# Down weights of all eight experts kept on the chip, addressed by a register of TensorE

## The reference

```
x = x + 0.5 * ffn(layernorm(x));  x = x + attn(layernorm(x));  x = x + 0.5 * ffn(layernorm(x))
x = x + 0.5 * experts(x);         x = x + linear_attn(x);      x = x + 0.5 * experts(x)

def experts(x):
    xn = x * rsqrt(mean(x * x, -1) + eps) * ln_w
    vals, idx = top_k(xn @ Wg + bg, 2)
    w = softmax(vals)                       # the two weights of each row
    for e in range(8):                      # out starts at 0
        y = (silu(xn @ W1a[e] + b1a[e]) * (xn @ W1b[e] + b1b[e])) @ W2[e] + b2[e]
        out += weight_of_e_in_row * y
```

## Time and profile before

| | |
|---|---|
| median of 3 runs | 887.13 us (885.59 to 891.52) |
| the profiled execution | 894.74 us |
| its span, first to last instruction | 892.9 us |
| TensorE busy | 676.6 us, 76% of the span |
| first expert layer, tile loop | about 502 to 642 us |
| second expert layer, tile loop | about 735 to 875 us |

### The profile page before, as it was taken

The page is one execution under the profiler, slowest core; times in us unless marked ns, Lnnn a source line. Parts: engine busy times, 40 slices in busy tenths (PEclk is TensorE's granted clock), DMA queues, the critical chain, the costliest instruction groups (busy, mean ns, idle before and its releaser), DMA issues.

```text
span 892.9 us, 13483 instructions
## 1 busy us (share of the span) xinstructions
PE 676.6 (76%) x4694; PEld 502.3 (56%) x4694; DVE 486.9 (55%) x1449; ACT 441.4 (49%) x867; POOL 331.9 (37%) x393
## 2 busy tenths in 40 slices
PE   4498897479999993387996498889639657988981
PEld 2266784312222242265896488778537656878870
DVE  7878749821111129877748245435557753444553
ACT  6365314589999978254306333323424642333440
POOL 1390312213223213361303546545340063656443
PEclk8589999779999998599997599989959877999996
DMA  8100000585000000000002745547230056655544
GB/s 338 45 0 1 1 1 1 189 268 206 2 1 1 1 1 4 0 1 1 1 1 54 245 150 169 167 146 216 73 94 1 1 142 217 195 159 173 173 145 150
DMA packets 35688, 83.36 MB, mean 93 GB/s; under 512 B 5025, under 2 KB 19873, under 8 KB 35105
## 3 DMA queue, kind: packets, MB, share of 16 engines
q1 hardware_dynamic: 30496, 71.87, 24.5%
q0 software_dynamic: 5120, 10.58, 4.2%
HBM read 65.62 MB, written 16.81 MB: 92 GB/s over the span
## 4 chain that ended last, share of the span: by engine, by line
PE 55%; DVE 21%; issue 10%; ACT 9%; DMA 3%; POOL 1%; SPq 0%; DVEq 0%; ACTq 0%
PE ps L1918 17%; PE ps L1929 8%; PE ps L1830 5%; PE ps L1599 3%; ACT arena L1410 3%; PE ps L1725 3%; PE ps L1813 3%; DVE arena L705 2%; PE ps L1697 2%; DVE arena L703 2%; PE ps L1706 1%; DVE stats L610 1%; DVE arena L782 1%; PE ps L1837 1%; PE ps L1905 1%
## 5 line engine op out<-in xcount | busy, mean ns | idle before, releaser
L1918 PE MATMUL ps<-arena 128*128 128x256 f32 (+1 forms) x768 | 165.6, 370 | 36.1 <-issue 33.0
L1918 PEld LDWEIGHTS ps<-arena 128*128 128x128 f32 x768 | 135.9, 206 | 56.5 <-issue 37.2
L1466 ACT ACTIVATE arena<-ps,arena 128x256 f32<-128x256 f32 (+1 forms) x192 | 83.6, 438 | 166.2 <-PE ps L1918 73.3
L955 DVE SCALAR_TENSOR_TENSOR arena<-ps,arena 128x256 f32<-128x256 f32 (+1 forms) x192 | 83.8, 439 | 126.7 <-ACT arena L1466 104.2
L1410 ACT ACTIVATE arena<-ps 128x512 f32<-128x512 f32 (+3 forms) x192 | 138.4, 827 | 4.5 <-PE ps L1813 3.2
L583 POOL DMA_INDIRECT yd<-arena,wq x80 | 78.6, 983 | 114.7 <-DVE arena L977 100.0
L547 POOL DMA_INDIRECT arena<-xs,wq x80 | 77.7, 971 | 31.3 <-issue 21.0
L1830 PE MATMUL ps<-arena 128*32 128x512 f32 (+3 forms) x768 | 83.6, 507 | 2.4 <-DVE arena L1188 1.6
L535 POOL TENSOR_SCALAR_AFFINE_SELECT arena<-arena 128x512 f32<-128x512 f32 x64 | 40.6, 634 | 115.0 <-ACT arena L1410 115.0
L1929 PE MATMUL ps<-arena 128*128 128x128 f32 x640 | 79.9, 276 | 2.0 <-DVE arena L977 2.0
L1929 PEld LDWEIGHTS ps<-arena 128*128 128x128 f32 x640 | 75.8, 193 | 2.5 <-issue 2.4
(11 more groups left out here) (295 smaller groups left out, 1288.0 us busy)
## 6 DMA issues: line engine op xcount, KB each, us to landing
arena<-in_wall SPq DMA_DIRECT2D x48, 836.0 KB
arena<-scr_q SPq DMA_DIRECT2D x8, 512.0 KB, 6.8
arena<-scr_k SPq DMA_DIRECT2D x8, 512.0 KB, 7.9
arena<-yd SPq DMA_DIRECT2D x8, 512.0 KB, 5.3
xs<-Xn SPq DMA_DIRECT2D x8, 260.0 KB, 4.9
scr_q<-arena SPq DMA_DIRECT2D x4, 384.0 KB, 4.5
scr_k<-arena SPq DMA_DIRECT2D x4, 384.0 KB, 3.9
arena<-xs,wq POOLq DMA_INDIRECT x80
```

The lines of the kernel that those rows point to most:

```text
L955: nc.vector.scalar_tensor_tensor(out=hT[:, j % 2, f, 0:rows], in0=ps[:, 3 + k % 3, 0:rows], scalar=raw[:, slot, EW_BB + f:EW_BB + f + 1], ...
L1466: nc.scalar.activation(sl[:, k % 3, 0:rows], ps[:, k % 3, 0:rows], ACT.Silu, bias=raw[:, slot, EW_BA + f:EW_BA + f + 1]).then_inc(sem("sil ...
L1918: ins = mm(ps[:, bank, 0:rows], raw[:, slot, w + P * f:w + P * (f + 1)], xTt[:, j % 2, 0:rows], start=True, stop=True)
```

## The change

The down weights of all eight experts leave the expert's load and are kept on the chip: one load of 128 x 4096 words (2 MB), at the start of the first expert layer, brings them into the last words of the arena (`kept`), where they stay for both layers. The load of each tile shrinks from 1672 to 1160 words for each partition (580 KB for 836 KB); the last bias stays in it. TensorE now reads the tile's expert from `tab` into a register of its own ahead of each down product and uses it in the address of the moving operand. It waits once a layer for the table and for the kept load. The semaphore `gatep` becomes the first count of `rank`.

```diff
-EW_A, EW_B, EW_2, EW_BA, EW_BB, EW_B2, EW = 0, 512, 1024, 1536, 1540, 1544, 1672
+EW_A, EW_B, EW_BA, EW_BB, EW_B2, EW = 0, 512, 1024, 1028, 1032, 1160
+EW_KEPT = 512
...
+        kept = arena[:, ARENA - E_ * EW_KEPT:ARENA].rearrange("p (e w) -> p e w", e=E_)
...
                 if not before:
                     sp.dma_start(route, a["route"]).then_inc(sem("route_in"), 16)
+                    sp.dma_start(kept[:, :, :], a["kept"]).then_inc(sem("kept_in"), 16)
                 sp.wait_ge(*at("expgap", i, 2))
...
-                gates(3).then_inc(sem("gatep", i), 1)
+                gates(3).then_inc(sem("rank", i), 1)
...
                 def down(j):
-                    slot = (before * NTILE + j) % WSLOT
+                    expert = pe.value_load(tab[0:1, j:j + 1], min_val=0, max_val=E_ - 1)
                     pe.wait_ge(*at("h", i, FT * (j + 1)))
                     if j:
                         pe.wait_ge(*at("y", i, j))
                     for h in range(TILES[j][1]):
                         for f in range(FT):
                             ins = mm(ps[:, 6, D * h:D * (h + 1)], hT[:, j % 2, f, P * h:P * (h + 1)],
-                                     raw[:, slot, EW_2 + D * f:EW_2 + D * (f + 1)], start=(f == 0), stop=(f == FT - 1))
+                                     kept[:, bass.ds(expert, 1), D * f:D * (f + 1)].rearrange("p o w -> p (o w)"), start=(f == 0), stop=(f == FT - 1))
                     ins.then_inc(sem("down", i), 1)
 
                 rows_in(0)
+                pe.wait_ge(*at("table", i, 1))
+                pe.wait_ge(sem("kept_in"), 16)
...
+    kept = z(P, E_, EW_KEPT)
...
-    wall[:, :, EW_2:EW_2 + FT * D] = f("L1_ffn_W2").reshape(E_, FT, P, D).transpose(2, 0, 1, 3).reshape(P, E_, FT * D)
+    kept[:, :, 0:FT * D] = f("L1_ffn_W2").reshape(E_, FT, P, D).transpose(2, 0, 1, 3).reshape(P, E_, FT * D)
```

More of the change, by code:

```diff
@@ L123 @@
                 nullv_in=16),
-    "moe": dict(gatep=1, pick=2, rank=2, columns=2, distance=len(PICK_ACT), act_rows=len(PICK_ACT), rows=4, index=2, counts=1, passed=7, expgap=2, mix=1, table=1,
+    "moe": dict(pick=2, rank=3, columns=2, distance=len(PICK_ACT), act_rows=len(PICK_ACT), rows=4, index=2, counts=1, passed=7, expgap=2, mix=1, table=1,
                 stored_rows=16 * NC, xtp=NTILE, xt=NTILE, up=NTILE * FT, silu=NTILE * FT, h=NTILE * FT,
@@ L873, in moe @@
                 backwards = over(route[:, RC_REV:RC_REV + E_], NT)
-                dve.wait_ge(*at("gatep", i, 1))
+                dve.wait_ge(*at("rank", i, 1))
                 link(nc.vector.tensor_tensor(lg, ps[:, 4, 0:NT * E_].rearrange("p (t e) -> p t e", t=NT),
@@ L895, in moe @@
                 nc.vector.tensor_tensor(mix[:, :, 1], mix[:, :, 0], gw[:, 1, :], ALU.mult).then_inc(sem("mix", i), 1)
-                dve.wait_ge(*at("rank", i, 1))
+                dve.wait_ge(*at("rank", i, 2))
                 rank_ = ps[:, 6, 0:NT * E_].rearrange("p (t e) -> p t e", t=NT)
@@ L936, in moe @@
                         ins.then_inc(sem("rows", i), 1)
-                dve.wait_ge(*at("rank", i, 2))
+                dve.wait_ge(*at("rank", i, 3))
                 nc.vector.tensor_copy(total, ps[:, 5, 0:COLS])
@@ L2096, in _layout @@
         "wall": wall,
+        "kept": kept,
         "route": route,
```

## The result

The changed kernel took 899.06 us (median of 4 runs, 896.9 to 901.5), the kernel before 886.36 us beside it: a ratio of 1.013, 95% interval 1.0099 to 1.0161. The forecast was 865, and the result lies above its range (850 to 893). The profiled execution took 896.9 us (span 895.1), only 2.2 us more than that of before, since it is one of the fastest of its kernel and the other lies above the four runs of its own. Besides, its trace has a head start of 2.9 us from steps in which nothing was changed: the route table's load starts at 467.37 us, before at 470.25. So the two traces show how the stages differ and the ratio shows by how much.

What follows compares the result with a forecast made beforehand. Bound: TensorE stalled on late signals, blamed on GpSimd transfers queued behind weight loads. Terms -23.4 - 5 + 0 + 0 + 6 = -22.4 us from 894.74 give 872.3; the runs' median, 7.6 lower, gives 865 us, range 850 to 893.

Steps and rivals of the forecast that it cites:

- The failing step: Wide tiles 4 to 16: shorter loads land transfers before GpSimd's fifth issue, so late signals stop; -23.4 us, ends -23.4 and 0.
- the run decides, not the bytes: Rival, wide tiles: GpSimd issuing more than four in a row makes signals late, however soon they land; 893 us, chance 0.17.
- The sentence against it: Against that rival: first gather's landing (5.09 us) and fifth issue (5.16) coincide so closely that bytes must matter.
- The layer starts: Start of each expert layer, six loads and 11 gathers competing: part of 11.6 us standing time goes; -5 us, ends -10.5 and 0.
- Narrow tiles by register work: Down products of 14 narrow tiles: register work exposes 0.3 to 0.5 us each; +6 us, between +1 and +11.
- Wide tiles hide it: Wide tiles' down products: 0.45 to 0.8 us of register work a tile is hidden behind 3.62 us of up product; no cost.
- the slower rival: Four matmuls of each down product: register addresses make them sent more slowly than the array takes them; 905 us, chance 0.11.
- The kept load: 2 MB load on SP's queue ahead of the sorted rows' stores: takes 7.8 us in an idle stretch, costs nothing.
- The merged semaphore: Merged semaphore and two waits ahead of the loop: a few tens of nanoseconds, counted as 0.

Runs made afterwards that it cites:

- late: Kind of comparison in which the kernel before takes 886 to 894 us, its trace showing stalls ahead of wide tiles' up products.
- few_bytes_2: Kernel before with weight loads of tiles 6 to 23 of each layer cut to 4 KB: 1.0052 late; as few_bytes, 0.9985 prompt.
- big_load: Changed kernel with each tile's load padded again to 836 KB, registers and kept weights as changed, against the kernel before: 1.0052 prompt.
- static_expert_2: Changed kernel with down product at expert 0's fixed address, no TensorE register work, against the kernel before: 0.9971 late; as static_expert, 0.9938 prompt.
- fewer_gathers: Kernel before with the second of two gathers left out in wide tiles 7 to 16, against the kernel before: 0.9729 late, 865.96 us.
- prompt: Kind of comparison in which the same kernel before takes 847 us; no trace of an edited kernel there has a wide-tile stall.
- early_one: Kernel before with EARLY = 1, SP waiting for tile 0's rows after one weight load, not two, against the kernel before: 0.9940 prompt.
- register_load_alone: Kernel before with an unused register load and its check ahead of each TensorE down product, against the kernel before: 1.0060 prompt.
- load_only: Changed kernel with register load kept but matmuls at expert 0's fixed address, against the kernel before: 1.0002 prompt; repeat 1.0023 late.
- hoisted_load_2: Changed kernel with the register load moved ahead of the next tile's up product, against the kernel before: 1.0079 late; earlier 0.9975 prompt.
- changed_fewer_gathers: Changed kernel without the second gather of wide tiles 7 to 16, against the kernel before: 1.0005 prompt; repeat 0.9734 late.

## Why the prediction was wrong

**The failing step** is in the first part of the change: "Then never more than three are out, and the late signals stop", the -23.4 us. Bytes do delay GpSimd's transfers (5.46 us against 3.66 for the first gather), but that delay doesn't make signals late. With loads of 4 KB the stalls stand (few_bytes_2), and with 836 KB loads and the same issues they can be absent (big_load). What the runs showed in its place: the stalls stay at 580 KB (27.9 us in tiles 2 to 16 for 23.7, and 21.4 in static_expert_2, where by the forecast nearly all should have gone), and those of the wide tiles go when GpSimd issues three transfers a tile and not four (fewer_gathers, 24 us). The rival "the run decides, not the bytes" was nearer. It isn't the whole of it: in prompt comparisons eleven issues in a row do no harm. The sentence against it, that landing and fifth issue coincide too closely, took 5.09 against 5.16 us for evidence, from a single gather. By the rule of the Trainium skill ("DMA: Bandwidth & Descriptors", "Queues, rings and completion order") that a DMA engine takes turns between its queues packet by packet I had put down that rival's time. The result (899 us) was nearer to that (893), though no run shows that it was for this reason: a gather did wait longer beside longer loads, 5.46 us for 3.66.

**The layer starts**, -5: about right as a sum, for another reason. The standing time after the first up product stayed (5.20 and 6.40 us before, 5.08 and 7.42 after in the timelines); the first gather landed 1.3 us earlier in the second layer's chain. static_expert (0.9938) puts the term at some 5 us, early_one (0.9940), which touches only when the first loads start, has as much. It goes with the loads' length: with the same register load on TensorE register_load_alone (836 KB) is at 1.0060 and load_only (580 KB) at 1.0002, both prompt. That the size was right is luck, since the reason given for it, fewer late signals, was wrong.

**Narrow tiles by register work**, +6: 14 x (3.50 - 3.06) = 6.2 us if every narrow tile pays it. In prompt traces tiles 17 to 22 of both layers, twelve of the fourteen, take 43.7 us (big_load) for 38.5 (few_bytes), 5.2 more: the term was right. The trace has 0.30 us for the load, 0.15 for the operation behind it and 0.046 for each of the four at the matmuls; I had estimated 0.27 to 0.48 and up to 0.165. The floor of about 600 ns that the Trainium skill gives for a loaded value ("DMA: Bandwidth & Descriptors", "Latency and other measured facts") is twice the 302 ns of this trace, which decides.

**Wide tiles hide it**: right where nothing is late (5.46 us in big_load with all register work), so the slower rival, matmuls that are sent too slowly, is refuted. Beside late signals it doesn't hold: 27.9 to 32.5 us lost against 21.4 for the fixed address, and 10.8 us between hoisted_load_2 and static_expert_2, whose narrow tiles without a stall are alike (3.07 and 3.06 us). That term, about 1% (1.0079 against 0.9971), stood at nothing in the prediction and was in no rival.

**The kept load**, 7.8 us and hidden: it took 7.9, in the idle stretch, and the stores behind it weren't held up. **The merged semaphore**: nothing of it shows.

**The sum as measured**, prompt: about -5 for the starts, +5 to 6 for the narrow tiles, 0 for the rest, and changed_fewer_gathers has 1.0005. Late: +12.7 us by the medians for a forecast of -22.4. The 23.4 us of stalls didn't go, and about 1% came on top of the prompt sum. In the traces of the three runs of the changed kernel the two tile loops, up to the last tile's up product, take 273.4, 278.8 and 280.5 us for 268.3: 4.1 to 8.7 us more in tiles 2 to 16, 1.4 to 4.7 in tiles 17 to 22, and 0.2 to 1.3 less in tiles 0 and 1. Each is one execution, so where the whole of the 1% lies isn't shown more closely.

**What stays open.** The traces show where late and prompt comparisons differ, but not what makes them differ. Rate, number in flight and bytes of GpSimd's transfers weren't told apart. And why register work lengthens the stalls was not settled; the operations wait for the loaded value and, as the order shows, for h and y too, so a signal that is late may be paid twice on TensorE's sequencer, but that is only argued. No kernel with fewer issues and the whole computation was run, so nothing here shows that the 24 us can be had.

## What to carry to other kernels

Idle time whose releaser the profile can't name should be tested by one kernel that takes the suspected cause away altogether, before a change is built on it: loads of four kilobytes in place of 836 settled here, in the first late comparison, what the traces could not. Ask also whether the stall is the kernel's own: compare executions from more than one occasion. A value loaded ahead of short work was paid in full (0.29 us on a tile of 3.06, 0.43 with the operations that use it), so it belongs one block of work earlier. The first transfer of a stage should share the engines with as few loads as the stage can bear: with one less it landed 2.1 us sooner (3.36 for 5.46 us), and the next tile's weights came 1.85 us late.

## What the hardware showed that was not expected

The same kernel ran at 847 or at 886 to 894 us, 5%, at mean granted clocks that are nearly alike (0.889 to 0.891 prompt, 0.883 to 0.885 late, the means of its runs in six of the comparisons). The difference lies in the expert layers' tile loops. The late trace of before (894.74 us) and the prompt one of few_bytes (847.67), which differs from it only in the bytes of later weight loads, are 47 us apart, and their loops 268.3 and 220.8: 24 us in tiles 2 to 16, 15 in tiles 0 and 1, 9 in tiles 17 to 22. With GpSimd's indirect transfers at four in 5.46 us tiles 2 to 16 can stall, at three they didn't in the two late traces there are. A register load on TensorE from the chip's own memory took 302 ns at the median, an operation on an address 46 ns.
